# Experts' gathered rows turned by transposing transfers of the sync engine instead of by TensorE transposes and a VectorE copy

## The chip, the cores and the metric

The kernel runs on one core of one Trainium2 chip. The metric is the device time of one execution in microseconds. Before the change it is 1390.61 us (median of 3 runs, 1389.44 to 1391.71).

## The reference, cut to what matters

A decoder layer on x of shape (4, 1024, 256), float32: linear attention over the sequence with 16 heads and a norm, a cross attention of 8 heads with 77 keys and a norm, and then a mixture of 8 experts, of which each of the 4096 tokens uses 4:

```python
router_logits = jnp.einsum('bsd,de->bse', x, router_w)
routing_weights = jax.nn.softmax(router_logits, axis=-1)
topk_weights, topk_indices = jax.lax.top_k(routing_weights, K)      # K = 4 of E = 8
topk_weights = topk_weights / jnp.sum(topk_weights, axis=-1, keepdims=True)
h = jnp.einsum('bsd,edh->bseh', x, up_w)                            # 256 -> 1024
h = jax.nn.gelu(h)
expert_outputs = jnp.einsum('bseh,ehd->bsed', h, down_w)            # 1024 -> 256
gathered = jnp.take_along_axis(expert_outputs, topk_indices[:, :, :, None], axis=2)
output = jnp.sum(topk_weights[:, :, :, None] * gathered, axis=2)
...
x = _layernorm(x + output, axis=-1)
```

## The kernel before, in words

`layer_kernel` calls three stages one after the other: `attention`, `experts`, `last_norm`. Each is a block in which every engine has a program of its own, written out by hand; nothing plans the order, and engines meet only at semaphores.

`attention` computes both attentions and the router. For every token it writes a row of 512 float16 numbers to DRAM (`token_rows`: 256 high parts and 256 low parts of the float32 value times 64, seen as 256 float32 words), the value itself to `token_sums`, and for each of the token's 4 experts a record (token index and routing weight) into that expert's region of `slot_records`. At its end `tile_tables` (L830 on) makes small tables on VectorE: the slots of each expert are cut into tiles of `SLOTS` = 256, there are at most `ETILES` = 71 tiles, and for tile t the tables give the expert (`tile_expert`), the first slot (`tile_slot`) and three scales. `past[:, t, e]` says whether tile t lies past the tiles of expert e-1, and `hot` is the difference of neighbours in it, a one-hot row that picks the expert's value.

`experts` (L1137 on) goes over the 71 tiles. For tile t:

- SyncE (SP) loads the tile's 256 records into a ring of `RING` = 8 buffers (L1186). It waits only until the ring's slot is free, that is until the results of tile t-8 were added (L1185).
- GpSimd (POOL) runs `gather(t)` (L1190 to L1197): two indirect DMAs of 128 rows of 1 KB each from `token_rows` into `xg`, which has two buffers. It waits until TensorE has turned the rows of tile t-2 (`xt_ready`). In GpSimd's order `result(t-3)` (L1199 to L1205) stands behind `gather(t)`: two indirect DMAs that add 128 rows of results each into `token_sums`. They wait for `y_ready` and for the adds of the tile before.
- TensorE (PE) runs `row_transposes(t)` (L1220 to L1227): 8 transposes of 128x128 float16 (4 groups of 128 numbers by 2 blocks of 128 rows) from `xg` into the PSUM tile `psx`. `up_products(t)` (L1232 to L1248) is 48 matmuls with 256 columns that read the turned rows `xT` and write `psu`, 4 groups of 12. `down_products(t)` (L1250 to L1263) is 48 matmuls that read `hh` and `hl` and write `psy`.
- ScalarE (ACT) applies the gelu, 4 instructions a tile from `psu` to `h` (L1286), and 2 instructions a tile from `psy` to `y` with the routing weight (L1294).
- VectorE (DVE) runs `take_rows(t)`: one copy of the turned rows from `psx` in PSUM to `xT` (L1308, two buffers of `xT`; it waits for `xt_ready` and, from tile 2 on, until `up_products(t-2)` has read the buffer), and the routing weights `gate` (L1313). `halves(t)` (L1315 to L1325) splits `h` into a high and a low float16 part, 8 instructions a tile.

The order on TensorE is written out:

```python
row_transposes(0)
up_products(0)
row_transposes(1)
for t in range(1, ETILES):
    up_products(t)
    if t + 1 < ETILES:
        row_transposes(t + 1)
    down_products(t - 1)
down_products(ETILES - 1)
```

`last_norm` loads `token_sums`, normalizes the rows and stores the output.

Of the kernel before, what the change touches and what calls it, by code (L numbers as in the profile page):

```python
# [7 lines left out]
F16 = mybir.dt.float16  # L8
# [7 lines left out]
P = 128  # L16
# [183 lines left out]
def attention(nc, k, rows, acc, slots, x, ctx, mask, Wq, bq, Wk, bk, Wv, bv, Wo, bo, ln_g, ln_b, xb, router, up, down):  # L200

    st = ExitStack()
    with st:
# [250 lines left out]
        def _(pool):  # L454
# [89 lines left out]
            for s in range(STEPS):  # L544
                c0, c1, c3, c4 = (chain_tile(s, d) for d in (0, 1, 3, 4))
                sends = record_sends(s)
                if c4 is not None:
                    inverse_deviation(2, c4)
                if c0 is not None:
                    inverse_deviation(0, c0)  # L550
                if s == 4:
                    pool.wait_ge(slots_cleared, 16 * (EXP * CAP // (P * INIT_SLOTS)))
                if c1 is not None:
                    inverse_deviation(1, c1)
                for b, half, t in sends:
                    scatter(b, half, t * TOPK, 2)
                if c3 is not None:
                    second_residual(c3)
                if chain_tile(s + 1, 1) is not None:
                    residual_bias(chain_tile(s + 1, 1))  # L560
                for b, half, t in sends:
                    scatter(b, half, t * TOPK + 2, 2)
                b, i = divmod(s - TB - 1, TB + 1)
                if i == 0 and 0 <= b < B:
                    mask_row(b)
                if s == STEPS - 2:
                    pool.wait_ge(tr_ready, TR["q", NT - 1] + 1)
                    pool.iota(io[:, :], pattern=[[1, ETILES]], base=0, channel_multiplier=0).then_inc(made, 1)
                    pool.iota(expi[:, :], pattern=[[CAP, EXP]], base=0, channel_multiplier=0).then_inc(made, 1)
                    pool.memset(past[:, :, 0:1], 1.0).then_inc(made, 1)  # L570
                    pool.memset(past[:, :, EXP:EXP + 1], 0.0).then_inc(made, 1)
                    pool.wait_ge(made, 1)
                    pool.tensor_copy(iof[:, :], io[:, :]).then_inc(made, 1)
                    pool.wait_ge(made, 2)
                    pool.tensor_copy(expert_slot[:, :], expi[:, :]).then_inc(made, 1)
# [92 lines left out]
        def _(dve):  # L668
# [159 lines left out]
            def tile_tables():  # L828
                n = [0]

                def done(ins):
# [1 line left out]
                    ins.then_inc(table_step, 1)  # L833
                    dve.wait_ge(table_step, n[0])

                dve.wait_ge(made, 6)
                dve.wait_ge(tr_ready, TR["q", NT - 1] + 1)
                dve.tensor_scalar(steps[:, :], iof[:, 0:PER], float(SLOTS), None, ALU.mult).then_inc(table_step, 1)
                dve.reciprocal(inv[:, :], k["wpow"][:, :]).then_inc(table_step, 1)
# [13 lines left out]
                                       steps[:, :].unsqueeze(1).to_broadcast([P, EXP, PER]), ALU.is_gt))  # L853
                done(dve.tensor_reduce(tiles[:, :], cmpt[:, :, :], AX_X, ALU.add))
                done(dve.tensor_tensor_scan(endt[:, :], ones[:, 0:EXP], tiles[:, :], 0.0, ALU.mult, ALU.add))
                done(dve.tensor_tensor(past[:, :, 1:EXP], iof[:, 0:ETILES].unsqueeze(2).to_broadcast([P, ETILES, EXP - 1]),
                                       endt[:, 0:EXP - 1].unsqueeze(1).to_broadcast([P, ETILES, EXP - 1]), ALU.is_ge))
                done(dve.tensor_reduce(te[:, :], past[:, :, 1:EXP + 1], AX_X, ALU.add))
                done(dve.tensor_tensor(hot[:, :, :], past[:, :, 0:EXP], past[:, :, 1:EXP + 1], ALU.subtract))
                done(dve.tensor_tensor(start[:, :], endt[:, :], tiles[:, :], ALU.subtract))  # L860
                done(dve.scalar_tensor_tensor(out=first[:, :], in0=start[:, :], scalar=-float(SLOTS), in1=expert_slot[:, :], op0=ALU.mult, op1=ALU.add))
# [275 lines left out]
def experts(nc, k, rows, acc, slots):  # L1137

    st = ExitStack()
    with st:  # L1140
# [14 lines left out]
        hl = sb("hl", [P, 2, HC, SLOTS], F16)  # L1155
        y = sb("y", [P, 2, SB, C])
        gate = sb("gate", [P, 2, SB])
        psx = [ps(f"psx{i}", [P, 1024], F16) for i in range(2)]
        psu = [ps(f"psu{i}", [P, 512]) for i in range(UBANKS)]
        psy = [ps(f"psy{i}", [P, 512]) for i in range(2)]  # L1160
        warm = sb("warm", [P, 1])
# [1 line left out]
        rec_loaded = [sem(f"rec_loaded{i}") for i in range(RING)]  # L1163
        xg_loaded = [sem(f"xg_loaded{i}") for i in range(2)]
        y_added = [sem(f"y_added{i}") for i in range(2)]
        xt_ready, xt_copied, up_ready, gelu_ready = sem("xt_ready"), sem("xt_copied"), sem("up_ready"), sem("gelu_ready")
        hh_ready, hl_ready, down_ready, y_ready = sem("hh_ready"), sem("hl_ready"), sem("down_ready"), sem("y_ready")
        gate_ready, table_loaded = sem("gate_ready"), sem("warm_ready")
        block = st.enter_context(nc.Block())

        def xtile(t):
            return psx[t % 2][:, 0:2 * CC * SLOTS].rearrange("p (q s) -> p q s", s=SLOTS)

        def ytile(t):
            return psy[t % 2][:, 0:SB * C].rearrange("p (j c) -> p j c", c=C)
# [3 lines left out]

        @block.sync  # L1180
        def _(sp):
            for t in range(ETILES):
                if t >= RING:
                    sp.wait_ge(y_added[t % 2], added(t - RING))
                at = sp.value_load(k["tile_slot"][0:1, t:t + 1], min_val=0, max_val=EXP * CAP - SLOTS)  # L1185
                sp.dma_start(rec[:, t % RING, :, :], slots[bass.ds(at, SLOTS), :].rearrange("(j p) w -> p j w", p=P)).then_inc(rec_loaded[t % RING], 16)  # L1186

        @block.gpsimd
        def _(pool):
            def gather(t):  # L1190
                if t >= 2:
                    pool.wait_ge(xt_ready, t - 1)
                pool.wait_ge(rec_loaded[t % RING], 16 * (t // RING + 1))
                for j in range(SB):
                    pool.indirect_dma_start(xg[:, t % 2, j, :], None, rows,  # L1195
                                            bass.IndirectOffsetOnAxis(ap=rec[:, t % RING, j, 0:1], axis=0)
                                            ).then_inc(xg_loaded[t % 2], 16)  # L1197

            def result(t):  # L1199
                pool.wait_ge(y_ready, SB * (t + 1))  # L1200
                if t >= 1:
                    pool.wait_ge(y_added[(t - 1) % 2], added(t - 1))
                for j in range(SB):
                    pool.indirect_dma_start(acc, bass.IndirectOffsetOnAxis(ap=rec[:, t % RING, j, 0:1], axis=0),  # L1204
                                            y[:, t % 2, j, :], None, compute_op=ALU.add).then_inc(y_added[t % 2], 16)  # L1205

            gather(0)
            gather(1)
            gather(2)
            for t in range(3, ETILES):  # L1210
                gather(t)
                result(t - 3)
            for t in range(ETILES - 3, ETILES):
                result(t)
            for t in (ETILES - 2, ETILES - 1):
                pool.wait_ge(y_added[t % 2], added(t))

        @block.tensor
        def _(pe):
            def row_transposes(t):  # L1220
                pe.wait_ge(xg_loaded[t % 2], 16 * SB * (t // 2 + 1))
                if t >= 2:
                    pe.wait_ge(xt_copied, t - 1)
                for q in range(2 * CC):
                    for j in range(SB):
                        ins = pe.transpose(xtile(t)[:, q, j * P:(j + 1) * P], xg[:, t % 2, j, q * P // 2:(q + 1) * P // 2].bitcast(F16), k["ident16"][:, :])  # L1226
                ins.then_inc(xt_ready, 1)  # L1227

            def expert_of(t):
                return pe.value_load(k["tile_expert"][0:1, t:t + 1], min_val=0, max_val=EXP - 1)  # L1230

            def up_products(t):  # L1232
                e = expert_of(t)
                pe.wait_ge(xt_copied, t + 1)
                w = k["wu"][:, bass.ds(e, 1), :, :, :].rearrange("p e s c h -> p (e s) c h")
                for g in range(NG):
                    use = NG * t + g
                    if use >= UBANKS:
                        pe.wait_ge(gelu_ready, use - UBANKS + 1)
                    for i in range(GRP):  # L1240
                        m = (GRP * g + i) * P
                        n = 0
                        for c in range(CC):
                            for ws, xs in ((0, 0), (0, 1), (1, 0)):
                                ins = pe.matmul(psu[use % UBANKS][:, i * SLOTS:(i + 1) * SLOTS], w[:, ws, c, m:m + P], xT[:, t % 2, xs * CC + c, :],  # L1245
                                                start=(n == 0), stop=(n == 3 * CC - 1))
                                n += 1
                    ins.then_inc(up_ready, 1)  # L1248
# [13 lines left out]
                            n += 1  # L1262
                    ins.then_inc(down_ready, 1)  # L1263

            row_transposes(0)
            up_products(0)
            row_transposes(1)
            for t in range(1, ETILES):
                up_products(t)
                if t + 1 < ETILES:  # L1270
                    row_transposes(t + 1)
                down_products(t - 1)
            down_products(ETILES - 1)

# [26 lines left out]

        @block.vector
        def _(dve):
            def take_rows(t):
                dve.wait_ge(xt_ready, t + 1)
                if t >= 2:
                    dve.wait_ge(up_ready, NG * (t - 1))
                dve.tensor_copy(xT[:, t % 2, :, :], xtile(t)).then_inc(xt_copied, 1)  # L1308

                dve.wait_ge(rec_loaded[t % RING], 16 * (t // RING + 1))  # L1310
                if t >= 2:
                    dve.wait_ge(y_ready, SB * (t - 1))
# [11 lines left out]
                    dve.wait_ge(hh_ready, use + 1)  # L1324
                    dve.scalar_tensor_tensor(out=lo, in0=h[:, use % UBANKS, :], scalar=k["h_scale"][:, t:t + 1], in1=hi, op0=ALU.mult, op1=ALU.subtract).then_inc(hl_ready, 1)  # L1325

            take_rows(0)
            halves(0)
            take_rows(1)
            for t in range(1, ETILES):  # L1330
                halves(t)
                if t + 1 < ETILES:
                    take_rows(t + 1)


def last_norm(nc, k, acc, out):
# [101 lines left out]
```

## Time and profile before

| What | us |
|---|---|
| Median of 3 runs | 1390.61 |
| The profiled execution: its own time | 1391.54 |
| The profiled execution: span from the first instruction to the last | 1389.8 |
| `attention`, up to the first record load of `experts` | 550.9 |
| TensorE busy over the span | 1182.6 |
| VectorE busy over the span | 803.6 |
| GpSimd busy over the span | 690.0 |
| ScalarE busy over the span | 483.4 |

The profiled execution took 1391.54 us, of which the span covers 1389.8; 1.7 us lie around it. Busy time of an engine is the union of its instructions. "PE" is TensorE's matmuls, "PEld" its weight loads, which run beside the matmuls. A matmul's recorded duration is longer than the step from one matmul to the next, since matmuls are pipelined. "PEclk" is the granted TensorE clock as a share of 2.4 GHz. "SPq" and "POOLq" mark DMAs that SyncE and GpSimd issue.

### The profile page before, as it was taken

What the parts mean: (1) busy time and instruction counts of PE and PEld (TensorE: products, weight loads), DVE (VectorE), ACT (ScalarE), POOL (GpSimd) and SP (SyncE); (2) the same over time, 40 slices, a digit from 0 to 9 for tenths busy, and PEclk for the clock granted to TensorE, in tenths of its full rate; (3) what the DMA queues carried; (4) which work ended last, traced back from release to release, by engine and by line L of the source; (5) the groups of instructions that cost most, each with busy time, mean ns of one, the idle gap of its engine ahead of it and who ended that gap; (6) DMA issues with size and microseconds to landing.
All of it is one profiled execution on the core that took longest, in us unless ns stands there. A gap on an engine that the chain in (4) does not pass through costs nothing. (4 is left out here: it accounts for less than half of the span.)

```text
span 1389.8 us, 28367 instructions
## 1 busy us (share of the span) xinstructions
PE 1182.6 (85%) x9258; PEld 986.2 (71%) x9258; DVE 803.6 (58%) x1897; ACT 483.4 (35%) x909; POOL 690.0 (50%) x784
## 2 busy tenths in 40 slices
PE   6688778888777750899999999999999999999950
PEld 3456556665565530799999999999999999999950
DVE  2468787778867733545555555555455555455516
ACT  2245444454524310233333333333333333333312
POOL 3024277477657765344555444544445554445423
PEclk9899899789877855899999999999999999999985
DMA  4113223223122210233333333333333333333327
GB/s 136 43 53 107 72 66 105 69 66 113 55 85 75 64 35 9 44 50 48 49 52 55 52 49 48 52 52 55 51 48 49 52 54 55 49 48 50 52 25 242
DMA packets 94900, 88.08 MB, mean 63 GB/s; under 512 B 32572, under 2 KB 87920, under 8 KB 94512
## 3 DMA queue, kind: packets, MB, share of 16 engines
q0 software_dynamic: 31360, 38.30, 17.4%
q1 hardware_dynamic: 63408, 47.96, 11.5%
q8 instruction: 90, 1.47, 0.4%
q14 instruction: 42, 0.34, 0.1%
HBM read 51.35 MB, written 34.87 MB: 62 GB/s over the span
## 5 line engine op out<-in xcount | busy, mean ns | idle before, releaser
L1204 POOL DMA_INDIRECT token_sums<-y,rec x142 | 235.9, 1661 | 367.8 <-ACT y L1294 343.3
L1245 PE MATMUL psu<-xT,w_up 128*128 128x256 f16 x3408 | 387.3, 274 | 3.2 <-DVE xT L1308 3.2
L1260 PE MATMUL psy<-w_down,hh 128*128 x2272 | 375.8, 273 | 0.0
L1245 PEld LDWEIGHTS psu<-xT,w_up 128*128 x3408 | 335.1, 98 | 44.0 <-issue 3.6
L1260 PE MATMUL psy<-w_down,hl 128*128 x1136 | 309.6, 273 | 0.0
L1286 ACT ACTIVATE h<-psu,up_scale 128x512 f32<-128x512 f32 x284 | 195.2, 687 | 175.7 <-PE psu L1245 175.6
L1260 PEld LDWEIGHTS psy<-w_down,hh 128*128 128x128 f16 x2272 | 219.4, 98 | 24.1
L1325 DVE SCALAR_TENSOR_TENSOR hl<-h,h_scale,hh 128x512 f16<-128x512 f32 x284 | 213.4, 752 | 10.2
L1294 ACT ACTIVATE y<-psy,gate 128x256 f32<-128x256 f32 x142 | 59.6, 471 | 359.9 <-PE psy L1260 359.9
L1313 DVE TENSOR_SCALAR gate<-rec,y_scale 128x2 f32<-128x2 f32 x71 | 16.4, 230 | 284.5 <-ACT y L1294 284.5
L1323 DVE TENSOR_SCALAR hh<-h,h_scale 128x512 f16<-128x512 f32 x284 | 138.8, 489 | 71.0 <-ACT h L1286 66.0
L1195 POOL DMA_INDIRECT xg<-token_rows,rec x142 | 140.2, 987 | 55.7 <-issue 42.4
L541 POOL DMA_INDIRECT slot_records<-recs,posi x128 | 130.5, 1020 | 40.2 <-issue 30.7
L1260 PEld LDWEIGHTS psy<-w_down,hl 128*128 128x128 f16 x1136 | 111.2, 98 | 12.9
L512 POOL TENSOR_SCALAR ve<-mv 128x1 f32<-128x1 f32 x96 | 24.3, 253 | 157.8 <-DVE mv L710 156.7
L1037 PE MATMUL big<-wqkv,xinT 128*128 128x512 f32 x128 | 71.1, 684 | 5.6 <-ACT xinT L591 5.6
L1226 PE MATMUL psx<-ident,xg 128*128 128x128 f16 x568 | 43.7, 220 | 32.6 <-DMA xg<-token_rows,rec 32.6
L525 POOL TENSOR_TENSOR X<-X 128x256 f32<-128x256 f32 x32 | 45.3, 1416 | 35.3 <-DVE L L952 26.2
L1226 PEld LDWEIGHTS psx<-ident,xg 128*128 128x128 f16 x568 | 37.9, 98 | 34.2 <-DMA xg<-token_rows,rec 32.7
L1308 DVE COPY xT<-psx 128x1024 f16<-128x1024 f16 x71 | 48.6, 684 | 21.5 <-PE psx L1226 21.5
L514 POOL TENSOR_TENSOR rstd<-ve,nhalf 128x1 f32<-128x1 f32 x96 | 56.8, 591 | 8.1 <-POOL ve L512 0.2
L1104 PE MATMUL small<-vx,pT 128*128 128x99 f32 (+2 forms) x320 | 49.0, 308 | 12.6 <-ACT pT L598 12.5
(208 smaller groups left out, 1411.1 us busy)
## 6 DMA issues: line engine op xcount, KB each, us to landing
w_down<-in_L_ffn_up_w_dram SPq DMA_DIRECT2D x8, 1024.0 KB, 5.4
w_down<-in_L_ffn_down_w_dram SPq DMA_DIRECT2D x7, 1024.0 KB, 5.7
XA<-in_x_dram SPq DMA_DIRECT2D x32, 128.0 KB, 2.3
XRES<-in_x_dram SPq DMA_DIRECT2D x32, 128.0 KB
token_sums<-X SPq DMA_DIRECT2D x32, 128.0 KB
token_rows<-XR SPq DMA_DIRECT2D x32, 128.0 KB, 1.7
sums<-token_sums SPq DMA_DIRECT2D x8, 512.0 KB, 7.4
out_dram<-sums SPq DMA_DIRECT2D x8, 512.0 KB, 3.0
```

Source lines behind the costliest of these rows:

```text
L514: pool.tensor_tensor(rstd[:, kind, at:at + 1], ve[:, kind, at:at + 1], nhalf[:, 0:1], ALU.pow).then_inc(rstd_ready[kind], 1)
L541: pool.indirect_dma_start(slots, bass.IndirectOffsetOnAxis(ap=posi[:, half, e:e + 1], axis=0), recs[:, half, e // TOPK, e % TOPK, :], None ...
L1037: pe.matmul(dst[:, 0:2 * C], xT[:, c, :], wqkv[:, c, C:3 * C], start=(c == 0), stop=(c == CC - 1))
L1195: pool.indirect_dma_start(xg[:, t % 2, j, :], None, rows, bass.IndirectOffsetOnAxis(ap=rec[:, t % RING, j, 0:1], axis=0)).then_inc(xg_load ...
L1204: pool.indirect_dma_start(acc, bass.IndirectOffsetOnAxis(ap=rec[:, t % RING, j, 0:1], axis=0), y[:, t % 2, j, :], None, compute_op=ALU.add ...
L1226: ins = pe.transpose(xtile(t)[:, q, j * P:(j + 1) * P], xg[:, t % 2, j, q * P // 2:(q + 1) * P // 2].bitcast(F16), k["ident16"][:, :])
L1245: ins = pe.matmul(psu[use % UBANKS][:, i * SLOTS:(i + 1) * SLOTS], w[:, ws, c, m:m + P], xT[:, t % 2, xs * CC + c, :], start=(n == 0), sto ...
L1260: ins = pe.matmul(ytile(t)[:, j, :], (hh, hl)[hs][:, t % 2, c, j * P:(j + 1) * P], w[:, ws, c, :], start=(n == 0), stop=(n == 3 * HC - 1))
L1286: act.activation(h[:, use % UBANKS, :], psu[use % UBANKS][:, :], ACT.Gelu_apprx_tanh, scale=k["up_scale"][:, t:t + 1]).then_inc(gelu_ready, 1)
L1294: act.activation(y[:, t % 2, j, :], ytile(t)[:, j, :], ACT.Copy, scale=gate[:, t % 2, j:j + 1]).then_inc(y_ready, 1)
L1323: dve.tensor_scalar(hi, h[:, use % UBANKS, :], k["h_scale"][:, t:t + 1], None, ALU.mult).then_inc(hh_ready, 1)
L1325: dve.scalar_tensor_tensor(out=lo, in0=h[:, use % UBANKS, :], scalar=k["h_scale"][:, t:t + 1], in1=hi, op0=ALU.mult, op1=ALU.subtract).the ...
```

## The change: what it does

The transposes on TensorE, their two PSUM tiles and the copy on VectorE are taken out. SyncE instead issues two transposing DMAs a tile, one for each block of 128 rows: each reads 128 partitions x 512 float16 of `xg` in SBUF and writes `xT` as 128 partitions x 4 groups x 128 rows. They wait until the rows of the tile are gathered and until `up_products(t-2)` is done with the `xT` buffer. `up_products(t)` and `gather(t+2)` now wait for these DMAs (`xt_loaded`). The record loads are issued 4 tiles ahead of the transposes instead of as far as the ring allows. In `tile_tables` the comparison now covers all 8 experts, so tiles past the last expert's have no hot entry (their scales are zero), and one memset on GpSimd goes.

```diff
@@ attention
-                    pool.memset(past[:, :, EXP:EXP + 1], 0.0).then_inc(made, 1)
...
-                dve.wait_ge(made, 6)
+                dve.wait_ge(made, 5)
...
-                done(dve.tensor_tensor(past[:, :, 1:EXP], iof[:, 0:ETILES].unsqueeze(2).to_broadcast([P, ETILES, EXP - 1]),
-                                       endt[:, 0:EXP - 1].unsqueeze(1).to_broadcast([P, ETILES, EXP - 1]), ALU.is_ge))
-                done(dve.tensor_reduce(te[:, :], past[:, :, 1:EXP + 1], AX_X, ALU.add))
+                done(dve.tensor_tensor(past[:, :, 1:EXP + 1], iof[:, 0:ETILES].unsqueeze(2).to_broadcast([P, ETILES, EXP]),
+                                       endt[:, :].unsqueeze(1).to_broadcast([P, ETILES, EXP]), ALU.is_ge))
+                done(dve.tensor_reduce(te[:, :], past[:, :, 1:EXP], AX_X, ALU.add))
@@ experts
-        psx = [ps(f"psx{i}", [P, 1024], F16) for i in range(2)]
...
+        xt_loaded = [sem(f"xt_loaded{i}") for i in range(2)]
...
         @block.sync
         def _(sp):
-            for t in range(ETILES):
+            def records(t):
                 if t >= RING:
                     sp.wait_ge(y_added[t % 2], added(t - RING))
                 at = sp.value_load(k["tile_slot"][0:1, t:t + 1], min_val=0, max_val=EXP * CAP - SLOTS)
                 sp.dma_start(rec[:, t % RING, :, :], slots[bass.ds(at, SLOTS), :].rearrange("(j p) w -> p j w", p=P)).then_inc(rec_loaded[t % RING], 16)
 
+            def turned_rows(t):
+                sp.wait_ge(xg_loaded[t % 2], added(t))
+                if t >= 2:
+                    sp.wait_ge(up_ready, NG * (t - 1))
+                for j in range(SB):
+                    sp.dma_start_transpose(xT[:, t % 2, :, j * P:(j + 1) * P], xg[:, t % 2, j, :].bitcast(F16)).then_inc(xt_loaded[t % 2], 16)
+
+            for t in range(4):
+                records(t)
+            for t in range(ETILES):
+                turned_rows(t)
+                if t + 4 < ETILES:
+                    records(t + 4)
...
             def gather(t):
                 if t >= 2:
-                    pool.wait_ge(xt_ready, t - 1)
+                    pool.wait_ge(xt_loaded[t % 2], added(t - 2))
...
-            def row_transposes(t):
-                pe.wait_ge(xg_loaded[t % 2], 16 * SB * (t // 2 + 1))
-                if t >= 2:
-                    pe.wait_ge(xt_copied, t - 1)
-                for q in range(2 * CC):
-                    for j in range(SB):
-                        ins = pe.transpose(xtile(t)[:, q, j * P:(j + 1) * P], xg[:, t % 2, j, q * P // 2:(q + 1) * P // 2].bitcast(F16), k["ident16"][:, :])
-                ins.then_inc(xt_ready, 1)
...
             def up_products(t):
                 e = expert_of(t)
-                pe.wait_ge(xt_copied, t + 1)
+                pe.wait_ge(xt_loaded[t % 2], added(t))
...
-            row_transposes(0)
             up_products(0)
-            row_transposes(1)
             for t in range(1, ETILES):
                 up_products(t)
-                if t + 1 < ETILES:
-                    row_transposes(t + 1)
                 down_products(t - 1)
...
-            def take_rows(t):
-                dve.wait_ge(xt_ready, t + 1)
-                if t >= 2:
-                    dve.wait_ge(up_ready, NG * (t - 1))
-                dve.tensor_copy(xT[:, t % 2, :, :], xtile(t)).then_inc(xt_copied, 1)
-
+            def gates(t):
                 dve.wait_ge(rec_loaded[t % RING], 16 * (t // RING + 1))
```

## Rows read from the trace of the kernel before

**Rows 1.** The busy time by stretch; the columns stand in the first row.

```profile
core 0: us, PE busy (x) PEld busy (x) DVE busy (x) ACT busy (x) POOL busy (x), PEclk, DMA share, GB/s
0.00:550.90 550.90, 402.25 (x1874) 285.46 (x1874) 373.70 (x1107) 219.40 (x466) 300.02 (x468) 0.82 0.24 72
600.00:1320.00 720.00, 720.00 (x6855) 648.40 (x6854) 378.48 (x659) 236.74 (x396) 348.74 (x263) 1.00 0.32 51
1350.00:1389.80 39.80, 0.00 (x0) 0.00 (x0) 21.47 (x80) 8.73 (x16) 13.86 (x32) 0.50 0.63 211
```

**Rows 2.** Waits from 600 to 1300: who, for whom, sum, times, longest.

```profile
ACT y L1294 <- PE psy L1260: 325.5, 64, 5.4
POOL token_sums L1204 <- ACT y L1294: 301.2, 64, 5.0
DVE gate L1313 <- ACT y L1294: 263.9, 64, 4.5
```

**Rows 3.** Timeline of TensorE's weight loads in one period: start, duration, what.

```profile
898.67 5.23 PEld L1245 LDWEIGHTS psu<-xT,w_up 128*128 x48
...
909.60 5.23 PEld L1245 LDWEIGHTS psu<-xT,w_up 128*128 x48
914.84 0.54 PEld L1226 LDWEIGHTS psx<-ident,xg 128*128 128x128 f16 x8
915.34 0.15 PEld L1260 LDWEIGHTS psy<-w_down,hh 128*128 128x128 f16 x2
...
920.52 1.52 PEld L1245 LDWEIGHTS psu<-xT,w_up 128*128 x14
```

**Rows 4.** The page's groups of the removed instructions: busy, mean ns, idle before.

```profile
L1226 PE MATMUL psx<-ident,xg 128*128 128x128 f16 x568 | 43.7, 220 | 32.6 <-DMA xg<-token_rows,rec 32.6
L1308 DVE COPY xT<-psx 128x1024 f16<-128x1024 f16 x71 | 48.6, 684 | 21.5 <-PE psx L1226 21.5
```

**Rows 5.** Timeline of the first two tiles of the stage.

```profile
557.20 0.77 PEld L1226 LDWEIGHTS psx<-ident,xg 128*128 128x128 f16 x8 [32.65 <-DMA xg<-token_rows,rec]
...
559.10 7.12 PEld L1245 LDWEIGHTS psu<-xT,w_up 128*128 x48 [1.13 <-issue]
...
566.24 0.54 PEld L1226 LDWEIGHTS psx<-ident,xg 128*128 128x128 f16 x8
...
568.46 0.68 DVE L1308 COPY xT<-psx 128x1024 f16<-128x1024 f16 x1
...
569.27 6.82 PEld L1245 LDWEIGHTS psu<-xT,w_up 128*128 x48 [2.50 <-issue]
```

**Rows 6.** Busy time by stretch around the first two tiles, columns as in rows 1.

```profile
562.50:566.20 3.70, 3.70 (x32) 3.21 (x31) 2.72 (x5) 1.45 (x3) 0.00 (x0) 0.90 0.02 4
...
569.30:572.50 3.20, 3.20 (x19) 2.32 (x20) 0.49 (x2) 0.69 (x1) 0.12 (x1) 0.62 0.16 54
572.50:576.10 3.60, 3.60 (x30) 3.05 (x29) 2.37 (x5) 1.37 (x2) 0.00 (x0) 0.87 0.00 0
576.10:590.00 13.90, 13.90 (x138) 12.54 (x136) 8.55 (x15) 4.28 (x7) 5.31 (x4) 1.00 0.21 29
```

**Rows 7.** Timeline of GpSimd in one period; the waiting time stands in brackets.

```profile
900.18 1.62 POOL L1204 DMA_INDIRECT token_sums<-y,rec  x1 [4.71 <-ACT y L1294]
902.10 1.71 POOL L1204 DMA_INDIRECT token_sums<-y,rec  x1 [0.30 <-issue]
904.11 1.01 POOL L1195 DMA_INDIRECT xg<-token_rows,rec  x1 [0.30 <-issue]
905.43 0.97 POOL L1195 DMA_INDIRECT xg<-token_rows,rec  x1 [0.30 <-issue]
911.10 1.62 POOL L1204 DMA_INDIRECT token_sums<-y,rec  x1 [4.71 <-ACT y L1294]
```

**Rows 8.** DMA issues from 520 to 1340: count, KB each, median us to landing.

```profile
xg<-token_rows,rec POOLq DMA_INDIRECT x142, 2.8
token_sums<-y,rec POOLq DMA_INDIRECT x140, 3.9
rec<-slot_records SPq DMA_DIRECT2D x71, 16.0 KB, 2.0
```

**Rows 9.** The queue SyncE feeds: packets, MB, share of 16 engines' span; 520 to 1340, then whole.

```profile
q1 hardware_dynamic: 19372, 1.21, 1.4%
...
q1 hardware_dynamic: 63408, 47.96, 11.5%
```

**Rows 10.** Issue durations of the record loads on SyncE, in ns, and their first and last start.

```profile
L1186 SPq DMA_DIRECT2D rec<-slot_records x71: 377/378/412, 550.9 to 1267.4; - x71
```

More of the change, by code:

```diff
@@ L1165, in experts @@
         y_added = [sem(f"y_added{i}") for i in range(2)]
-        xt_ready, xt_copied, up_ready, gelu_ready = sem("xt_ready"), sem("xt_copied"), sem("up_ready"), sem("gelu_ready")
+        xt_loaded = [sem(f"xt_loaded{i}") for i in range(2)]
+        up_ready, gelu_ready = sem("up_ready"), sem("gelu_ready")
         hh_ready, hl_ready, down_ready, y_ready = sem("hh_ready"), sem("hl_ready"), sem("down_ready"), sem("y_ready")
@@ L1169, in experts @@
         block = st.enter_context(nc.Block())
-        def xtile(t):
-            return psx[t % 2][:, 0:2 * CC * SLOTS].rearrange("p (q s) -> p q s", s=SLOTS)
         def ytile(t):
@@ L1325, in halves @@
                     dve.scalar_tensor_tensor(out=lo, in0=h[:, use % UBANKS, :], scalar=k["h_scale"][:, t:t + 1], in1=hi, op0=ALU.mult, op1=ALU.subtract).then_inc(hl_ready, 1)
-            take_rows(0)
+            gates(0)
             halves(0)
-            take_rows(1)
+            gates(1)
             for t in range(1, ETILES):
@@ L1332, in _ @@
                 if t + 1 < ETILES:
-                    take_rows(t + 1)
+                    gates(t + 1)
 def last_norm(nc, k, acc, out):
```

## The prediction

> **What bounds the kernel now.** Read the busy time by stretch first [rows 1]: from 600 to 1320 TensorE is busy for 720.00 of 720 us at full granted clock (1.00, that is 2.4 GHz), while VectorE has 378.48, ScalarE 236.74 and GpSimd 348.74. A busy PE alone proves little, so read the waits second [rows 2]: in that stage ScalarE waits for TensorE, and GpSimd and VectorE wait for ScalarE; TensorE has no wait in the list. So the experts' stage lasts as long as TensorE's instruction stream, and the attention stage (550.90 us) and the last 39.80 us, with no matmul in them, are not touched by the change.
>
> The timeline of weight loads gives the steps of that stream [rows 3]. Up products run from 909.60 to 914.84 (5.24 us), the 8 transposes take the place from 914.84 to 915.34 (0.50 us), down products run from 915.34 to 920.52 (5.18 us), and the period is 10.92 to 10.93 us (898.67 to 909.60). There are 71 tiles.
>
> **Removed on TensorE.** The group of the transposes says 43.7 us busy, 220 ns each [rows 4]. That is not what they cost: durations of pipelined matmuls overlap, and the step counts. By the steps it is 0.50 us for 8, 63 ns each, in each of the 69 tiles from 2 to 70: 69 x 0.50 = 34.5 us, all on the path, if the turned rows are there when the up products want them. The Trainium skill (TensorE: Matmul & The Clock Gate, Part 4: PE-mode transpose) has about 275 ns a transpose within a kernel, which over 568 would promise 156 us; the duration of 220 ns in the row is near it, but the step of 63 ns decides, and it gives a quarter of that.
>
> **The first two tiles.** Today tile 1's transposes start at 566.24, its copy waits in VectorE's order behind the halves of tile 0 until 568.46, and its up products start at 569.27 [rows 5]. That gap of 3.03 us goes, since nothing of VectorE stands there any more. The gap also costs clock: the granted clock was 0.90 and rising before it, 0.62 in the 3.20 us after it, 0.87 in the next, then 1.00 [rows 6], and up products of tile 1 took 6.82 us instead of 5.23 [rows 3, 5]. Without the gap I count these 1.6 us as won too (bounds 0 and 1.6; I take 1.6, since the clock had already come up within tile 0). For tile 0 the way from landed rows to the first up product is today 559.10 - 557.20 = 1.9 us [rows 5]; afterwards it is D, the time from landed rows of a tile to both its transposing DMAs landed.
>
> **What D is.** No row of before shows a transposing DMA. From below: SyncE issues a DMA in 378 ns [rows 10], the nearest one lands in 2.0 us [rows 8], and a tile's 256 KB, if they move as 1024 pieces of 256 B (one row's share of one output group) at the cheapest price of a packet on this queue, add a little. That price: 1.4% of 16 x 820 us over 19372 packets is 9.5 ns for 62 B; over the whole span 11.5% of 16 x 1389.8 over 63408 is 40 ns for 756 B [rows 9]. So 1024 pieces on 16 engines are 0.6 to 2.6 us, and D is 2 x 0.38 + 2.0 + 0.6 = 3.4 to 5.4 us. From above: if the write side goes in runs of 16 numbers (32 B), 8192 pieces at 9.5 to 40 ns are 4.9 to 20.5 us, so D 8 to 23; if it goes number by number, 131,072 pieces are at least 78 us. I take D = 5, nearest to the gathers, which move the same bytes in 1 KB rows and land in 2.8 us each [rows 8].
>
> **How much D may be.** Count from the start U of up(t-1), 898.67. ScalarE's results let GpSimd go at 900.18; two adds and two gathers follow, the second gather is issued at 905.43 [rows 7] and lands 2.8 us later, at 908.2: U + 9.56. Those are the rows of tile t+1 (today turned at 914.84). Its xT buffer is free from 903.9, earlier. Its up products should start two periods after U, at 2 x 10.42 = 20.84 without transposes. So D up to 11.3 us is hidden. At D = 5 there are 6 us to spare. Above it two periods are 9.56 + D: the period is (9.56 + D)/2, and the old 10.93 comes back at D = 12.3.
>
> **Other edits.** VectorE's copy (684 ns, 48.6 us in all [rows 4]) lies beside TensorE's work in every tile but 0 and 1, where it is counted above: nothing more. VectorE keeps its other waits, and its 378.48 of 720 us leave it cover. GpSimd's gather of tile t+2 now waits for xt_loaded(t), and the adds of tile t-1 stand behind it in its order; but xt_loaded(t) is there before up(t) starts at 909.60, and that gather comes at 915.05 by the adds ahead of it (911.10 + 1.62 + 0.3 + 1.7 + 0.3 [rows 7]), so the wait ends first: nothing. On SyncE the record load of tile t+4 stands behind the waits for the rows of tile t and for up(t-2), and is issued about three periods before its gather; it lands in 2.0 us [rows 8]: nothing. At the start four loads instead of eight precede (378 ns each), and SyncE then waits for rows anyway. Two transposing DMAs and one record load a period are all that SyncE issues, 3 x 0.38 = 1.1 us of 10.4 by the record load's duration [rows 10]. The DMA engines are at 0.32 share [rows 1]; 256 KB more in, by the prices above, add at most 0.25 in the likely case. An add lands in 3.9 us [rows 8] and the next add waits for it 9 us later [rows 7], so it can be 5 us late and cost nothing. The comparison in tile_tables is one eighth longer, one instruction, once; a memset goes: nothing. Tiles past the last expert's now load records of another place with scales of zero, the same work.
>
> **Sum,** against the profiled execution of 1391.54 (span 1389.8 and 1.7 around it): -34.5 (69 tiles) - 3.03 - 1.6 (tile 1) + (5 - 1.9) (tile 0) = -36.0, so 1355.5. The median of the runs is 0.93 below that execution, so I say 1354.6. By D from 3.4 to 11.3 it is 1353 to 1361; without the 1.6 of clock 1.6 more.
>
> **Rivals.**
> A. D is 11.3 to 13 us: the wait moves from nothing to `xt_loaded` in front of each up(t), and the gain is eaten. At D = 12 the period is 10.78 and the sum 1391.5 - 69 x 0.15 - 4.6 + 10.1 = 1387; at 12.3 it is about 1397. For it: the trace has no such DMA, and 32 B runs give 8 and more. Against it: that needs three times the landing of a gather of the same bytes. The Trainium skill (VectorE: DVE Perf Modes, The three transpose paths) has 1309 ns for one 128x128 block through a DMA. A tile has 8 blocks, so an estimate by that page is 10.5 us if they run one after another: hidden with 0.8 us to spare in each period, and 5.5 us dearer at tile 0, about 1360. That is the rule that speaks against this change; it leaves the gain standing but thin.
> B. Slower: the transposing DMAs are the bound. Place: TensorE waits for `xt_loaded` in front of every up(t). It decides from D = 12.3. At D = 16 the period is 12.8 and the time 1391.5 + 69 x 1.85 + 9.5 = 1529; at the 23 us of 32 B runs with the dear packet price, 16.3 and about 1780; number by number over 3700. For it: the price is unknown and small pieces are dear per byte. Against it: the 64 B pieces of record loads on the same queue cost only 9.5 ns each.
> C. The transposing DMAs get in the way of the adds and gathers on the same 16 engines, so that gathers land late: 5 us later landing eats the spare time of D = 5 and costs nothing; only beyond that does it pass into A. It would need an add's landing to go from 3.9 to over 9 us. Its price is that of A.
> D. The stage was not bound by TensorE's stream, and removed steps come back as waits for ScalarE or VectorE: 1389 to 1391. Against it: VectorE works 378.48 / 720 x 10.93 = 5.7 us a period, ScalarE 3.6 [rows 1], and their waits all lead to TensorE.
>
> **Chances.** The forecast (D up to 11.3) 0.81, A 0.06, B 0.10, C 0.01, D 0.02. A measurement of this kernel tells about 0.2% (2.8 us) from no change. Faster takes the forecast and most of A and C: 0.85; same takes D and the rest of A: 0.04; slower 0.11. The range: low is D = 3.4 with 2 us for what I have not seen, 1351; high reaches into A, 1370.
>
> **What would show it.** Right: the period by weight loads of L1245 is 10.4 us, down products follow up products with no gap, TensorE has no wait from 600 to 1300, the granted clock there is 1.00, up of tile 1 follows tile 0 directly in about 5.2 us, the two DMAs land within 11 us of the gather. Wrong: waits for `xt_loaded` in TensorE's rows (A, B); adds landing in 8 us or more (C); a period of 10.9 with waits for ScalarE (D); a first tile that starts more than 5 us later than 559.10 says that D was mis-sized.

## The result, and the profile after

After the change the kernel takes 1359.57 us (median of 4 runs, 1358.55 to 1360.28), before 1391.07 (4 runs, 1389.44 to 1391.71). The ratio is 0.9769, 95% interval 0.9755 to 0.9784: 31.5 us less. The forecast was 1354.6 (1351 to 1370), so the direction was right, the time lies in the range, and the gain was forecast 5 us too large. Whether the cause was right is for the experiments to say. The profiled execution took 1359.07 us, its span is 1357.2, that is 32.6 us under the span before.

The busy time by stretch of the changed kernel, the columns as in [rows 1]:

```profile
0.00:550.90 550.90, 402.43 (x1874) 285.45 (x1874) 373.41 (x1107) 219.21 (x466) 299.84 (x467) 0.82 0.24 72
600.00:1200.00 600.00, 600.00 (x5499) 537.79 (x5497) 293.93 (x514) 205.84 (x345) 303.47 (x229) 1.00 0.48 78
```

TensorE is still busy throughout at the full granted clock, and the attention stage is the same to 0.2 us of TensorE's work. The DMA share rose from 0.32 to 0.48, and VectorE, without its copy, fell from 0.53 of the stretch (378.48 of 720 us) to 0.49. The waits from 600 to 1300 again have no line of TensorE's [rows 2]:

```profile
ACT y L1291 <- PE psy L1261: 310.8, 67, 4.9
POOL token_sums L1214 <- ACT y L1291: 287.6, 67, 6.8
DVE gate L1305 <- ACT y L1291: 285.8, 67, 4.6
```

The timeline of weight loads answers to [rows 3]: the period is 10.48 us, not 10.42 as forecast.

```profile
893.87 5.23 PEld L1246 LDWEIGHTS psu<-xT,w_up 128*128 x48
904.35 5.23 PEld L1246 LDWEIGHTS psu<-xT,w_up 128*128 x48
914.83 5.23 PEld L1246 LDWEIGHTS psu<-xT,w_up 128*128 x48
```

The missing 0.05 us was in the trace of before, in a view the prediction didn't use, TensorE's matmuls instead of its weight loads:

```profile
909.70 5.40 PE L1245 MATMUL psu<-xT,w_up 128*128 128x256 f16 x48
914.94 0.61 PE L1226 MATMUL psx<-ident,xg 128*128 128x128 f16 x8
915.39 0.38 PE L1260 MATMUL psy<-w_down,hh 128*128 x2
...
920.63 0.60 PE L1245 MATMUL psu<-xT,w_up 128*128 128x256 f16 x4
```

From matmul start to matmul start the transposes take 915.39 - 914.94 = 0.45 us, 56 ns each, and both kinds of products 5.24. A weight load runs ahead of its matmul, and not by the same time at both ends of the group: the transposes' first load (914.84) stands 0.10 us before its matmul, the first load of the down products (915.34) only 0.05 us. So the step between these two loads is 0.05 us longer than the step between the matmuls, and the down products looked 0.05 us shorter, 5.18 instead of 5.24 [rows 3]. The Trainium skill (TensorE: Matmul & The Clock Gate, Part 1) gives 55.6 ns from start to start for 128 columns at the full clock; this trace agrees with 56.

Around the first two tiles, SyncE's, GpSimd's and TensorE's rows after [rows 5]:

```profile
553.01 0.99 POOL L1205 DMA_INDIRECT xg<-token_rows,rec  x1 [6.07 <-DMA rec<-slot_records]
554.30 0.97 POOL L1205 DMA_INDIRECT xg<-token_rows,rec  x1 [0.30 <-issue]
...
557.06 2.62 SPq L1189 DMA_TRANSPOSE xT<-xg  x2
560.70 0.40 SPq L1182 DMA_DIRECT2D rec<-slot_records  x1
...
561.05 13.45 PE L1246 MATMUL psu<-xT,w_up 128*128 128x256 f16 x96 [36.38 <-DMA xT<-xg]
...
574.33 0.38 PE L1261 MATMUL psy<-w_down,hh 128*128 x2
```

The rows of tile 0 land at 557.06 and its up products start at 561.05: D was 4.0 us. Tile 1's up products follow with no gap (96 matmuls in one row). But from the first of them to the first down product it is 13.28 us, not the 10.48 that two times 48 products take at the full clock: the granted clock was 0.50 for the first 3.45 us and 0.67 in the next 3.5.

```profile
561.05:564.50 3.45, 3.45 (x17) 2.45 (x18) 0.00 (x0) 0.68 (x1) 1.89 (x2) 0.50 0.58 122
564.50:568.00 3.50, 3.50 (x23) 2.69 (x22) 2.10 (x4) 0.71 (x3) 1.58 (x2) 0.67 0.26 60
568.00:574.40 6.40, 6.40 (x61) 5.74 (x59) 5.82 (x11) 3.42 (x5) 0.40 (x1) 1.00 0.33 76
```

What the new DMA costs its issuer, and what the queue's packets took from 600 to 1200 (share of 16 engines' time):

```profile
L1189 SPq DMA_TRANSPOSE xT<-xg x116: 1197/1242/2635, 599.5 to 1199.2; - x116
```

```profile
q1 hardware_dynamic: 78061, 16.03, 15.7%
```

Each holds SyncE 1.24 us, three times a record load [rows 10]. The record loads made 1.5% of that share before, so the 116 DMAs took 14.2% of 9600 engine-us, 11.7 each, or 0.73 us of all 16 engines. That is 539 packets a DMA at 22 ns, between the 9.5 and 40 ns of the bounds, and near the 512 pieces of 256 B that were assumed.

### The profile page after: what moved, and what is told of

The parts are those of the page before. It is cut to its first block and busy times, and to the rows that moved or that the text cites. A ratio compares the mean times of both kernels' runs of the same rounds, so it can differ in the third digit from the quotient of the medians.

```text
span 1357.2 us, 27232 instructions
## 1 busy us (share of the span) xinstructions
PE 1149.5 (85%) x8690; PEld 953.7 (70%) x8690; DVE 760.5 (56%) x1826; ACT 483.1 (36%) x909; POOL 690.2 (51%) x783
## 5 line engine op out<-in xcount | busy, mean ns | idle before, releaser
L1246 PE MATMUL psu<-xT,w_up 128*128 128x256 f16 x3408 | 386.3, 274 | 36.4 <-DMA xT<-xg 36.4
L1261 PEld LDWEIGHTS psy<-w_down,hh 128*128 128x128 f16 x2272 | 222.3, 98 | 25.7
L1103 PEld LDWEIGHTS small<-vx,pT 128*128 128x128 f32 (+1 forms) x320 | 44.1, 216 | 18.9 <-ACT pT L597 16.4
L1070 PE MATMUL small<-woT,zT 128*128 128x256 f32 x128 | 41.8, 457 | 12.7 <-DVE wcl L687 6.4
L1093 PE MATMUL big<-kbd,x1T 128*128 128x308 f32 x128 | 51.3, 485 | 0.0
```

Source lines behind the costliest of these rows:

```text
L1103: ins = pe.matmul(dst[:, h0 * (XD + 1):h1 * (XD + 1)], pT[0:n, c, :], vx[0:n, c, 0:h1 - h0, :].rearrange("p h d -> p (h d)"), start=(c == ...
L1261: ins = pe.matmul(ytile(t)[:, j, :], (hh, hl)[hs][:, t % 2, c, j * P:(j + 1) * P], w[:, ws, c, :], start=(n == 0), stop=(n == 3 * HC - 1))
```

## The experiments

Medians carry the scatter of the attention stage, which ends at times up to 8 us apart in the profiled executions. So each run is also read "by the stage": from ScalarE's table load, its first instruction in `experts`, to the end of the span. That is one profiled execution of each run. The ratios are against the kernel before, run beside each on the same chip. Code is cut to the lines that matter; "..." marks a cut. The table load of the changed kernel:

```profile
549.93 1.28 ACT L1275 ACT_TABLE_LOAD   x1 [28.28 <-PEq L203]
```

| Run | Median us | Ratio to before, interval | Stage to end of span, us |
|---|---|---|---|
| before | 1391.07 | | 1389.8 - 549.9 = 839.9 |
| after | 1359.57 | 0.9769 (0.9755 to 0.9784) | 1357.2 - 549.9 = 807.3 |
| e1 | 1389.95 | 0.9994 (0.9984 to 1.0004) | 838.7 |
| e2 | 1357.11 | 0.9762 (0.9742 to 0.9782) | 807.3 |
| e3 | 1359.09 | 0.9771 (0.9755 to 0.9787) | 807.6 |
| e4 | 1362.18 | 0.9789 (0.9773 to 0.9805) | 810.0 |
| e5 | 1527.82 | 1.0984 (1.0967 to 1.1000) | 979.9 |
| e6 | 1899.03 | 1.3659 (1.3638 to 1.3680) | 1345.6 |
| e7 | 1356.34 | 0.9752 (0.9733 to 0.9771) | 806.2 |
| e8 | 1357.53 | 0.9767 (0.9753 to 0.9781) | 804.7 |
| e9 | 1405.97 | 1.0118 (1.0097 to 1.0139) | 850.4 |
| e10 | 1354.86 | 0.9740 (0.9727 to 0.9754) | 803.4 |
| e11 | 1360.22 | 0.9773 (0.9760 to 0.9786) | 807.4 |
| e12 | 1354.98 | 0.9740 (0.9727 to 0.9754) | 803.4 |

**e1, TensorE's transposes back, their result unused.**

```diff
...
+            row_transposes(0)
             up_products(0)
+            row_transposes(1)
             for t in range(1, ETILES):
                 up_products(t)
+                if t + 1 < ETILES:
+                    row_transposes(t + 1)
```

> The changed kernel with TensorE's 8 transposes a tile put back at their old place in its order, into PSUM tiles that nobody reads; the up products still read what the transposing DMAs wrote. Theory (the gain is TensorE's stream, 0.45 us a tile by matmul starts, and the DMAs are hidden): the period goes from 10.48 back to 10.93, and the time up by 69 x 0.45 + 0.5 = 31.5 us to 1391 us, within 1.5. Rival 1 (the gain came from VectorE, freed of the copy and its waits): it stays at 1360 us. Rival 2 (the DMAs cost TensorE or GpSimd something that lessened the gain): over 1393, since both are paid.

Measured 1389.95 us, by the stage 31.4 us more than after. The period is back at 10.92 (next row 10.93 later):

```profile
579.12 5.41 PE L1256 MATMUL psu<-xT,w_up 128*128 128x256 f16 x48
584.36 0.61 PE L1237 MATMUL psx<-ident,xg 128*128 128x128 f16 x8
590.04 5.40 PE L1256 MATMUL psu<-xT,w_up 128*128 128x256 f16 x48
```

So all but 1.2 us of the gain hangs on the place of 8 transposes in TensorE's stream. Rival 1 is out. The rest of the change (the tables, the order of record loads, VectorE's copy, the DMAs) is worth 839.9 - 838.7 = 1.2 us, and it lies in tiles 0 and 1: from the landed rows to the end of tile 1's up products it is 573.43 - 555.66 = 17.8 us here and was 19.0 before.

**e2, VectorE's copy back.**

```diff
...
             def gates(t):
+                dve.wait_ge(copied, t + 1 if t else 2)
+                dve.tensor_copy(xcopy[:, t % 2, :], psx[t % 2][:, :].bitcast(F16)).then_inc(copied, 1)
```

> The changed kernel with VectorE's copy of 128x1024 float16 from PSUM put back once a tile at its old place in VectorE's order; it copies constants into a buffer that nobody reads. Theory: VectorE has 4 us a period to spare, so 1360 us, within 1; at tiles 0 and 1 at most 1 us more. Rival 1 (the gain came from VectorE): the period goes back to 10.9 and the time to 1385 to 1391 us.

Measured 1357.11, by the stage 807.3, the same as after to 0.1 us. The median is 2.5 us lower. In the profiled execution (1354.78 us) the attention stage, which the edit doesn't touch, ended 4.3 us earlier (table load at 545.66); the four runs lie from 1354.77 to 1359.95. VectorE's busy time went up, and TensorE is still busy throughout:

```profile
600.00:1200.00 600.00, 600.00 (x5499) 536.78 (x5497) 330.31 (x575) 205.78 (x344) 305.30 (x230) 1.00 0.47 78
```

**e3, the transposing DMAs of tiles 2 to 70 left out.**

```diff
             def turned_rows(t):
+                if t >= 2:
+                    return
...
```

The waits for these DMAs go with them; the gather of tile t waits for the gather of tile t-2 instead.

> The changed kernel without the transposing DMAs of tiles 2 to 70: all later up products read the turned rows of tiles 0 and 1 (the turning of the others is left out), the gathers and adds run as before. Theory: the 138 DMAs left out were hidden and disturb nobody, so 1360 us, within 1. Rival 2 (contention of the DMAs with the adds, the gathers or the matmuls' reads): faster by more than 2 us, with a period under 10.48.

Measured 1359.09, by the stage 807.6. The DMA share falls back to 0.33 and the time stays within 0.3 us, so the two DMAs a tile of tiles 2 to 70 cost the kernel nothing that can be seen:

```profile
600.00:1200.00 600.00, 600.00 (x5499) 537.78 (x5498) 294.95 (x516) 206.23 (x345) 304.43 (x230) 1.00 0.33 53
```

**e4, four transposing DMAs a tile.**

```diff
+                for r in range(TURNS - 1):
+                    for j in range(SB):
+                        sp.dma_start_transpose(xs[:, t % 2, r, :, j * P:(j + 1) * P], xg[:, t % 2, j, :].bitcast(F16)).then_inc(xt_loaded[t % 2], 16)
                 for j in range(SB):
                     sp.dma_start_transpose(xT[:, t % 2, :, j * P:(j + 1) * P], xg[:, t % 2, j, :].bitcast(F16)).then_inc(xt_loaded[t % 2], 16)
...
```

> The changed kernel with the two transposing DMAs of every tile preceded by two more of the same rows into a scratch buffer, on the same semaphore. Each DMA holds SyncE 1.25 us, so D is 4.0 + 2.5 = 6.5 us. Theory (hidden up to D = 11.3): the period stays 10.48; tile 0 pays 2.5 us, so 1362 us, within 1.5. Rival 2 (DMA traffic costs by its amount): the period rises, at 0.1 us each by 7 us or more, to 1367 or above.

Measured 1362.18, by the stage +2.7. All of it is at tiles 0 and 1: D at tile 0 is 6.6 us (558.90 to 565.48), and the period stays at 10.48. From 600 to 1200 TensorE is busy throughout, with the DMA share at 0.63:

```profile
600.00:1200.00 600.00, 600.00 (x5498) 536.87 (x5497) 295.45 (x516) 205.09 (x343) 304.61 (x230) 1.00 0.63 103
```

**e5 and e6, eight and twelve DMAs a tile** (the same edit, `TURNS` 4 and 6).

> As e4, with six extra transposing DMAs a tile into scratch buffers, eight in all. D is 8 x 1.25 + 1.5 = 11.5 us. Theory 1 (the predicted bound: the period is (9.56 + D)/2 once D is over 11.3): a period of 10.5, tile 0 pays 7.5 us and tile 1 some, so 1367 to 1371 us. Theory 2 (SyncE's own queue is the first bound, since it issues all of one tile before it looks at the next: 8 x 1.25 + 1.0 to the record load + 0.4 = 11.4 to 11.5 us a period): 1359.6 + 69 x 0.95 + 8 = about 1433 us, with TensorE waiting for xT in every tile.

> As e5, with twelve transposing DMAs a tile. D is 16.5 us. Theory 1 (latency around two buffers): a period of (9.56 + 16.5)/2 = 13.0, about 1360 + 69 x 2.55 + 13 = 1549 us. Theory 2 (SyncE's queue): a period of 12 x 1.25 + 1.4 = 16.4, about 1360 + 69 x 5.9 + 13 = 1780 us.

Measured 1527.82 and 1899.03 us: slower than before by 9.8% and 36.6%. Theory 1's periods (10.5, 13.0) are out; theory 2 names the right queue and its periods (11.4, 16.4) are low, they are 12.9 and 18.0 from 600 to 1200. The waits of SyncE's own queue in 600 us of each:

```profile
SPq L1192 <- DMA xg<-token_rows,rec: 6.0, 3, 2.5
```

```profile
SPq L1183 <- DMA token_sums<-y,rec: 0.4, 1, 0.4
```

SyncE waits for almost nothing: issuing is all it does. In e5 the DMA engines are also at a share of 0.89 and single issues take up to 3.2 us, so there the issue time may itself hold a wait for the engines; in e6 the share is 0.69. Its timeline in e6 has 12 DMAs in 13.57 + 2.58 us, a pause of 1.0 and the record load; TensorE waits for what they write:

```profile
917.11 0.39 SPq L1184 DMA_DIRECT2D rec<-slot_records  x1
917.60 13.57 SPq L1192 DMA_TRANSPOSE xs<-xg  x10
931.21 2.58 SPq L1194 DMA_TRANSPOSE xT<-xg  x2
934.84 0.39 SPq L1184 DMA_DIRECT2D rec<-slot_records  x1
```

```profile
PE psu L1251 <- DMA xT<-xg: 174.1, 33, 7.7
```

**e9, six DMAs a tile** (`TURNS` 3).

> As e4, with six transposing DMAs a tile. The theory after e5 and e6: the bound is SyncE's own queue, which there took 12.9 us a period for 8 DMAs and 17.7 for 12, about 1.33 us a DMA and 1.6 around the record load in e5. For 6 DMAs that is 9.5 us, under the 10.48 of TensorE, so the period stays 10.48 and only the start pays: 1359.6 + 4 x 1.3 and some wait at tile 1, 1366 to 1369 us. Rival (the DMA engines, at 0.89 share in e5, slow the adds and gathers before SyncE is full): over 1380 us.

Measured 1405.97, 1.2% slower than before: my theory fell, and the rival's number held. SyncE is near full but not full (it waits 51.2 us in 600 for gathered rows), yet TensorE waits for turned rows. The wait of SyncE's queue:

```profile
SPq L1192 <- DMA xg<-token_rows,rec: 51.2, 30, 4.1
```

The place with the longest of TensorE's waits there, SyncE's, GpSimd's and TensorE's rows:

```profile
905.16 5.14 SPq L1192 DMA_TRANSPOSE xs<-xg  x4
910.35 2.69 SPq L1194 DMA_TRANSPOSE xT<-xg  x2
...
911.72 0.97 POOL L1210 DMA_INDIRECT xg<-token_rows,rec  x1 [0.30 <-issue]
...
918.25 5.22 SPq L1192 DMA_TRANSPOSE xs<-xg  x4
...
918.72 6.87 PE L1251 MATMUL psu<-xT,w_up 128*128 128x256 f16 x48 [3.00 <-DMA xT<-xg]
```

```profile
905.16:913.04 7.88, 7.88 (x74) 7.05 (x73) 5.14 (x9) 3.58 (x6) 5.31 (x4) 1.00 0.80 125
913.04:918.25 5.21, 2.68 (x25) 2.16 (x22) 0.23 (x1) 0.84 (x2) 1.30 (x1) 1.00 0.81 70
```

The last transposing DMA was issued by 913.04 and landed at 918.7, 5.7 us later (at tile 0 of the changed kernel the last one landed 1.4 us after its issue ended, 559.68 to 561.05). The gather issued at 911.72 landed at about 918.2, after 6.5 us instead of 2.8 [rows 8]. In these 5 us the engines were 0.81 busy and moved 70 GB/s, against 125 in the stretch before, so the same busy time moved about half the bytes. From the start of its tile's issues (905.16) to 918.72 it is 13.6 us, where six issues of 1.25 and a landing of 1.5 would be 9.0. So landings stretch before SyncE's queue is full. Whether the adds to DRAM beside the transposes do it, the turning itself, or another mix of packets, no run here tells; it stays open.

**e7, the clock kept up.**

```diff
...
+            for i in range(80):
+                pe.matmul(psu[UBANKS - 1][:, 0:SLOTS], k["wu"][:, 0, 0, 0, 0:P], k["wu"][:, 0, 0, 0, 0:SLOTS], start=True, stop=True)
             up_products(0)
```

> The changed kernel with 80 matmuls of weights by weights (256 columns, result unused) on TensorE ahead of the first up products, in time in which it waits for the rows. Theory (the first two tiles run part of their 96 matmuls at the half clock after the wait, 13.28 us from the first up product to the first down product instead of 10.48): the granted clock is up by 561 and the time falls by 2.8 us to 1356.8. Rival (the clock falls whatever TensorE did before, or the extra matmuls last beyond 561 and delay the stage): 1359.6 or up to 1362 us.

Measured 1356.34, but by the stage only 1.1 us less than after. The clock part held: 96 up products took 10.9 us in place of 13.28, with a short wait for tile 1's rows between.

```profile
548.13 10.36 PE L1267 MATMUL psu<-w_up 128*128 128x256 f16 x80 [25.33 <-PEq L203]
560.37 5.41 PE L1246 MATMUL psu<-xT,w_up 128*128 128x256 f16 x48 [1.88 <-DMA xT<-xg]
566.03 5.41 PE L1246 MATMUL psu<-xT,w_up 128*128 128x256 f16 x48 [0.25 <-DMA xT<-xg]
```

That is 2.4 us less; 1.2 of it went to tile 0's rows, which landed 8.3 us after the table load (548.09 to 556.41) instead of 7.1. Why the gather took longer isn't settled.

**e8 and e10, tile 0 turned by TensorE.** The edit of e10; e8 has 48 instead of 64 and not the 9 behind the transposes. Tiles 1 to 70 are turned by the DMAs; the waits that count them are adapted.

```diff
...
+            for i in range(64):
+                pe.matmul(psu[UBANKS - 1][:, 0:SLOTS], k["wu"][:, 0, 0, 0, 0:P], k["wu"][:, 0, 0, 0, 0:SLOTS], start=True, stop=True)
+            pe.wait_ge(xg_loaded[0], added(0))
+            for q in range(2 * CC):
+                for j in range(SB):
+                    ins = pe.transpose(psx[:, (q * SB + j) * P:(q * SB + j + 1) * P], xg[:, 0, j, q * P // 2:(q + 1) * P // 2].bitcast(F16), k["ident16"][:, :])
+            ins.then_inc(xt_ready, 1)
+            for i in range(9):
+                pe.matmul(psu[UBANKS - 1][:, 0:SLOTS], k["wu"][:, 0, 0, 0, 0:P], k["wu"][:, 0, 0, 0, 0:SLOTS], start=True, stop=True)
             up_products(0)
...
+            dve.wait_ge(xt_ready, 1)
+            dve.tensor_copy(xT[:, 0, :, :], psx[:, :].rearrange("p (q s) -> p q s", s=SLOTS)).then_inc(xt_copied, 1)
             gates(0)
```

> The changed kernel with 48 such matmuls, and tile 0 turned by TensorE and copied by VectorE as before the change, tiles 1 to 70 by the transposing DMAs. Theory: tile 0's rows reach the up products 1.7 us after they land instead of 4.0, and these run at the full clock: 2.3 + 2.8 = 5 us less than the changed kernel, 1354.5 us. Rival (the clock drops again in the wait for the copy, or tile 1's rows come late): only 0 to 2.5 us less.

> As e8, with 64 matmuls of weights ahead of the wait for tile 0's rows and 9 more between its transposes and its up products, so that TensorE does not stand still while VectorE copies. Theory (in e8 the clock fell again after the two gaps of 1 us: granted 0.51 from 563.5 to 567): the 96 matmuls of tiles 0 and 1 take 10.5 instead of 12.2 us, and from the start of the stage to the end of the span it is 803 us (after the change 807.3, e8 804.7), 1355 us in all. Rival (the clock falls anyway): as e8.

e8 measured 1357.53, by the stage -2.6; its rival held, the clock fell after the two gaps, in which TensorE stood for 1.0 us each:

```profile
563.50:567.00 3.50, 3.50 (x20) 2.51 (x18) 0.69 (x2) 0.69 (x1) 0.95 (x1) 0.51 0.63 150
```

e10 closes both gaps and measured 1354.86, by the stage -3.9 (expected 803, got 803.4): the clock stays at 1.00 and the 96 matmuls take their 10.5 us. That is 2.8 of the 3.9 us; the other 1.1 is the earlier start, 10.0 us after the table load (550.00 to 560.00) instead of 11.1. The transposes follow the 64 matmuls with no gap, so the trace doesn't show whether the rows had landed earlier and fewer matmuls would have done better.

```profile
558.52 0.61 PE L1284 MATMUL psx<-ident,xg 128*128 128x128 f16 x8
558.97 1.15 PE L1287 MATMUL psu<-w_up 128*128 128x256 f16 x9
560.00 10.65 PE L1258 MATMUL psu<-xT,w_up 128*128 128x256 f16 x96
```

**e11 and e12, the changed kernel and e10 once more on one chip.**

> The changed kernel as it is, on the same chip as the next one. 1359.6 us as before, within 2; from the start of the stage to the end of the span 807.3 us, within 0.5, wherever the attention stage ends.

> The kernel of e10 again. By the stage, which does not carry the scatter of the attention stage, 803.4 us within 0.5, so 4 us under the changed kernel on the same chip. Rival: e10's median was low because its attention stage happened to be short; then the two medians lie within 1 us.

1360.22 and 1354.98 us, ratios 0.9773 and 0.9740 with intervals that don't meet; by the stage 807.4 and 803.4. e10's kernel beats both kernels of this case, the changed one by 5 us in the median and by 4 by the stage. The rival of e12 (medians within 1 us) is out.

## Why the prediction was right, and where it was not

- **TensorE's stream is the bound, and the transposes' place in it is the gain: shown.** e1 puts them back and loses 31.4 of the 32.6 us again; e2 and e3 move nothing. Rival D is out.
- **The term 69 x 0.50 = 34.5 us was mis-sized.** It is 69 x 0.447 = 30.8 (matmul starts of tiles 2 to 69 before, 581.90 to 1313.99 over 67 periods, are 10.927; after, 579.57 to 1271.25 over 66, 10.480). The step was read from weight loads, which run ahead of their matmuls by 0.10 us at one end of the group and 0.05 at the other. It is 3.7 of the 5 us. A step was still the right reading: the row's busy time says 43.7 us [rows 4]. The 275 ns a transpose of the Trainium skill (TensorE: Matmul & The Clock Gate, Part 4) would have said 156 us, and the trace doesn't bear that out as a cost.
- **Tiles 0 and 1: forecast -1.5 us, measured -1.75** (from landed rows to the end of tile 1's up products 576.22 - 557.20 = 19.02 before, 574.33 - 557.06 = 17.27 after). That these agree is luck, two errors cancel: D was 4.0 and not 5, and the low clock cost 0.9 us more than counted. Before, the clock was 0.50 for the first 3.4 us of tile 0's up products and 0.90 after; now it was 0.50 and then 0.67. TensorE stood longer ahead of them (36.4 us, before 32.6 and then the transposes at 557.20), but that this is the reason is not shown.
- -30.8 - 1.75 is -32.6, all of the span's change. The other 1.4 us of the miss is the step from a profiled execution to a median: before, it lay 0.93 above the median of three; after, 0.5 below the median.
- **D from 3.4 to 5.4 held (4.0); its make-up did not.** I gave SyncE 0.38 us an issue, it takes 1.24; the landing behind it is 1.4, not 2.6. The two errors cancel at two DMAs and no longer at four: e4's D was 6.6, where the forecast's make-up gives 4 x 0.38 + 2.0 + 1.2 = 4.7.
- **D up to 11.3 us is hidden: held at 4.0 and 6.6 (e3, e4), not tested near 11.3; as a rule for more DMAs it failed.** With D put at 9.0 for six DMAs and 11.5 for eight it promises about no cost a period. e9 lost 0.6 us a tile with six, e5 2.4 with eight. The rule took D and the 2.8 us of a gather as fixed. They are not: at e9's place D was 13.6 and the gather 6.5, so that place doesn't refute the 11.3, only the count of D. It also left out that the issuing queue serves tiles one after another (e6). The change has room for twice its DMAs (e4), not three times.
- **C (the DMAs disturb adds and gathers) costs nothing at two and four DMAs a tile (e3, e4), and is the likely first limit at six (e9), which is not shown.** A and B did not come, since D was 4.0 and not over 11.3. The 1309 ns that the Trainium skill has for one block (VectorE: DVE Perf Modes, The three transpose paths) would make D 10.5 as an estimate; the trace has 4.0 for eight blocks.

## What to carry to other kernels

When one engine's stream is the bound, an instruction is worth the step from its start to the next start, read from the matmuls and not from the weight loads or the busy time; check it at both ends of the group. Moving work to a DMA queue cost nothing here only while three things had room: the latency to the deadline, the issuing engine's time for all tiles in turn, and the DMA engines' share; doubling the moved work in a test shows the room. Where single runs scatter by more than the effect, compare the stage alone.

## What the runs showed of the hardware

- A transposing DMA of 128 x 512 float16 from SBUF to SBUF holds SyncE 1.24 us, makes 539 packets of 22 ns, and two of them land 4.0 us after the first is issued. With eight a tile (e5) a single issue took up to 3.2 us.
- Two idle gaps of 1 us on TensorE (e8) were followed by a granted clock of 0.51 from 563.5 to 567, though it had been at 1.00 from 556.9 to 563.5; with the gaps filled (e10) it stayed at 1.00.
- In e9 DMA engines that were 0.81 busy moved about half of what they moved in the stretch before (70 against 125 GB/s), with landings of 5.7 and 6.5 us.
- The attention stage, the same code in all of these kernels, ended between 545.7 and 553.6 us, while the rest of the changed kernel took 807.3 to 807.6 in four runs (the changed kernel twice, e2, e3).
